# Attention on one core: value products of the fifth step moved into the sixth

## The reference

```python
qkv = jnp.einsum('bnc,dc->bnd', x, qkv_w) + qkv_b
...
attn = jnp.einsum('bhqd,bhkd->bhqk', q, k) * scale
attn = jax.nn.softmax(attn, axis=-1)
out = jnp.einsum('bhqk,bhkd->bhqd', attn, v)
```

## Time and profile before

| | |
|---|---|
| median of 3 runs | 4660.69 us (4658.37 to 4661.96) |
| the profiled execution | 4660.65 us, of which the span is 4658.9 us |
| dense stage | to 1320 us of the span |
| attention groups | 1321 to about 4484 us |
| granted TensorE clock | 0.996 of full speed over the span |

### The profile page before, as it was taken

How to read it: one execution, slowest core, us unless ns; L and a number is a source line. 1 busy time by engine, 2 the same in 40 slices (tenths; PEclk the granted TensorE clock), 3 DMA queues, 4 the chain that set the end, 5 groups by cost and what they waited for, 6 DMA issues and landing times.

```text
span 4658.9 us, 65600 instructions
## 1 busy us (share of the span) xinstructions
PE 4623.1 (99%) x24396; PEld 2958.7 (64%) x24396; DVE 3206.6 (69%) x5313; ACT 2392.8 (51%) x4649; POOL 3176.1 (68%) x1105
## 2 busy tenths in 40 slices
PE   8999999999999999999999999999999999999999
PEld 7888888888755555555555555555555555555567
DVE  5233233333388888888888888888888888888854
ACT  2112121121146666666666666666666666666631
POOL 1121212121268999999999999999999999999910
PEclk9999999999999999999999999999999999999999
DMA  5334353434346666566666666665666666666557
GB/s 176 108 118 138 95 163 93 133 117 135 104 100 135 131 138 135 130 136 135 132 139 133 132 136 134 136 135 128 138 137 132 135 135 132 138 133 136 120 181 259
DMA packets 263425, 629.23 MB, mean 135 GB/s; under 512 B 46788, under 2 KB 83652, under 8 KB 224712
## 3 DMA queue, kind: packets, MB, share of 16 engines
q0 software_dynamic: 36288, 264.26, 27.9%
q1 hardware_dynamic: 226824, 360.85, 27.5%
HBM read 224.96 MB, written 134.74 MB: 77 GB/s over the span
## 4 chain that ended last, share of the span: by engine, by line
PE 62%; POOL 5%; DMA 3%; issue 2%; ACT 1%; DVE 0%; POOLq 0%; DVEq 0%
PE st_ps L1493 20%; PE o_ps L1419 18%; PE mx_ps L1407 18%; POOL p_pair L1121 4%; PE mx_ps L1433 3%; PE st_ps L1441 3%; DMA p_pair<-p_pair 3%; PE mx_ps L1441 1%; ACT p_sb L1197 1%; POOL p_pair L1159 0%; PE mx_ps L1412 0%; POOL o_inv L1115 0%; POOL p_pair L1125 0%; ACT front L1207 0%; DVE y_in L1286 0%
## 5 line engine op out<-in xcount | busy, mean ns | idle before, releaser
L1232 DVE TENSOR_REDUCE unit_max<-mx_ps 128x1 f32<-128x512 f32 x4016 | 2456.4, 682 | 311.1 <-PE mx_ps L1407 309.0
L1197 ACT ACTIVATE p_sb<-st_ps 128x512 f32<-128x512 f32 x4096 | 2063.3, 628 | 860.4 <-PE st_ps L1493 860.3
L1121 POOL TENSOR_TENSOR p_pair<-p_sb 128x2048 f32<-128x2048 f32 x504 | 2433.5, 4875 | 6.7 <-PE mx_ps L1433 3.4
L1419 PE MATMUL o_ps<-p_sb,v_sb 128*32 128x512 f32 x8192 | 986.7, 599 | 0.0
L358 POOL TENSOR_TENSOR h_lo<-h_f,h_hi 128x512 fp32r<-128x512 f32 x128 | 165.3, 1291 | 709.1 <-DVE h_hi L576 709.1
L1419 PEld LDWEIGHTS o_ps<-p_sb,v_sb 128*32 128x32 f32 x8192 | 214.1, 109 | 433.9 <-issue 286.2
L426 ACT ACTIVATE h_f<-rot,b_sb 128x512 f32<-128x512 f32 x128 | 88.1, 689 | 656.0 <-PE rot L627 655.9
L1493 PE MATMUL st_ps<-q_x,k_x 97*128 97x512 f32 x1024 | 401.0, 413 | 1.8 <-ACT p_sb L1197 1.4
L1493 PE MATMUL st_ps<-front 97*128 97x512 f32 x1024 | 399.3, 410 | 1.1 <-ACT p_sb L1197 1.1
L1493 PE MATMUL st_ps<-q_x,front 97*128 97x512 f32 x1024 | 399.1, 410 | 0.0
L1493 PE MATMUL st_ps<-front,k_x 97*128 97x512 f32 x1024 | 398.6, 410 | 0.0
(11 more groups left out here) (124 smaller groups left out, 5922.2 us busy)
## 6 DMA issues: line engine op xcount, KB each, us to landing
p_pair<-p_pair POOLq DMA_DIRECT2D x252, 1024.0 KB, 7.6
xt<-x SPq DMA_DIRECT2D x64, 256.0 KB, 2.7
stage<-w SPq DMA_DIRECT2D x32, 512.0 KB, 4.2
q_hi_d<-qk_hi SPq DMA_DIRECT2D x64, 256.0 KB, 3.1
q_lo_d<-qk_lo SPq DMA_DIRECT2D x64, 256.0 KB, 3.6
k_hi_d<-qk_hi SPq DMA_DIRECT2D x64, 256.0 KB, 2.7
k_lo_d<-qk_lo SPq DMA_DIRECT2D x64, 256.0 KB, 3.4
v_d<-v_out SPq DMA_DIRECT2D x64, 256.0 KB, 2.3
```

The lines of the kernel that those rows point to most:

```text
L1121: pool.tensor_tensor(p_pair[:, slot, :, :], p_sb[:, n % SLOTS, :, :], p_sb[:, (n + 1) % SLOTS, :, :], ALU.add).then_inc(pair_done, 1)
L1197: act.activation(p_sb[:, (L * G * KT + n) % SLOTS, h, :], st_ps[bank(g, m)][:, :], ACT.Exp, scale=SCALE).then_inc(exp_done, 1)
L1232: dve.reduce_max(unit_max[:, n // 4, n % 4:n % 4 + 1], mx_ps[UNIT_PLACE[n] % RING][:, :], AX.X).then_inc(bank_read, 1)
L1419: op = pe.matmul(o_ps[rows, :], v_sb[u][:, kt, rows], p_sb[:, (L * G * KT + n) % SLOTS, h, :], start=(kt == 0), stop=(kt == KT - 1))
```

## The change

Two edits. In `STEPS` the strings of j = 4 and j = 5 are new: step 4 has no V any more and alternates U and S throughout; step 5 keeps its V after four U, and behind it the order is U S S U U S U S S where it was S S U S U U S U S. In `products`, the V of a step whose predecessor has none takes four key tiles (for j = 5: 6 to 9) where the others take two. Nothing is added or taken away, and no wait is of another kind.

```diff
         STEPS = ["USUSUSUVSSUSUUSUS", "USUSUSUVSSUSUUSUS", "USUSUSUVZSSUSUUSUS", "USUSUSUVZSSUSUUSUS",
-                 "USUSUSUVSSUSUUSUS", "USUSUSUVSSUSUUSUS", "USUSUSUVTSSUSUUSUS", "USUSUSUVZSSUSUUSUS"]
+                 "USUSUSUSUSUSUSUS", "USUSUSUVUSSUUSUSS", "USUSUSUVTSSUSUUSUS", "USUSUSUVZSSUSUUSUS"]
...
-                            for kt in (2 * j - 2, 2 * j - 1):
+                            for kt in range(2 * j - (2 if "V" in STEPS[j - 1] else 4), 2 * j):
                                 values(L, g * KT + kt, u, kt)
```

## The result

The changed kernel takes **4704.05 us** (median of 4 runs, 4702.46 to 4704.57), the kernel before 4661.32 us: a ratio of 1.0091, 95% interval 1.0077 to 1.0106. It is 0.9% slower, by 42.7 us; +36.3 us, 4697.0, was the forecast. The profiled execution has a span of 4702.8 us, 43.9 more than before.

The account below looks back on a forecast made before the run. PE's order was taken to bound the kernel; −0.38 + 1.06 − 0.02 = +0.66 us in 63 groups (+41.6), −0.4 for the last group and −4.9 from POOL gave +36.3, 4697.0 us; range 4683 to 4708, 8 times in 10.

Parts of the forecast that it names:

- The bound: In the attention, PE's order of work sets the pace, 49.24 us a group.
- The switch, −0.38 us: At step 4's removed visit, one entry and exit between whole-array and 32-column matmuls is saved, 0.38 us per group.
- Sixteen units, +1.06 us: Between the visits of steps 3 and 5, unit 16 waits for DVE's reduce 12, holding PE 1.06 us per group.
- Behind the long visit, −0.02 us: From step 5's visit to step 6's, the first unit goes two places earlier, the last leaves the edge: −0.02 us.
- What POOL gives back, −4.9 us: Over the attention, PE's longer period gives POOL room, so late joins no longer hold ACT and then PE: −4.9 us.
- The −0.4 us of the last group: The last group has output products instead of units and only saves the switch: −0.4 us.
- A: In steps 4 and 5 the four banks absorb DVE's lag, only the switch counts: faster, 4636 us; chance 5%.
- B: POOL sets the group's period and the extra PE time vanishes in PE's waits: no change, 4661 us; chance 4%.
- C: Key tiles 8 and 9 meet POOL 1.6 us earlier and it stands in their way: 4714 us; chance 6%.

Follow-up runs that it names:

- a_oldtail: Changed kernel with the order behind step 5's visit put back to S S U S U U S U S; 4697.74 us, ratio 1.008.
- b_short: Kernel before with DVE's unit reduces reading 256 of 512 columns and the exponential's scale a hundredth; 4647.26 us, ratio 0.9971.
- b_unit2nd: Kernel before with the first unit and second score behind the visit swapped in all eight steps; 4650.26 us, ratio 0.9976.
- a_short: Changed kernel with DVE's unit reduces reading 256 of 512 columns and the exponential's scale a hundredth; 4642.38 us, ratio 0.9962.
- b_early: Kernel before with S U S U U S U S S behind the visit in all eight steps; 4676.08 us, ratio 1.0028.

## Why the prediction was right

*The bound.* PE's order sets the period. Right: every change of a step on PE came out in the time, until the period fell to about 49.0 us, where late joins at step 2 took part of the gain.

*The switch, −0.38 us.* Right. With the old order behind the visit, steps 4 and 5 of `a_oldtail` are 0.67 us longer than before, and with a hold of 1.04 that leaves 0.37 for the switch. It holds 0.03 us that are not the switch but the edge of the ring at the eighth unit: the prediction took that wait to be without a loss, and `b_short` and `b_unit2nd` show that it was not. `a_short` against `b_short` shows only −0.26, since PE waits for ACT there in two places.

*Sixteen units, +1.06 us.* Right, with 1.04 between short and full reduces, 1.05 by the starts of the two units and of the visit, and 11.53 us for 448 columns, as expected. The wait at the eighth unit in the earlier trace rows, only 0.20 us and next to free, was the row that told it.

*Behind the long visit, −0.02 us.* This is the term that was mis-sized: it is +0.06, by `a_oldtail` against after (49.89 and 49.95). The prediction weighed where the first unit stands and not where the five scores stand, though it had the banks of `st_ps` and ACT's 0.49 us in hand. It is 0.08 us off, and the hold 0.02 the other way: a typical group is 0.71 us longer and not 0.66, which is 63 × 0.05 = 3 of the missing 6.4 us.

*What POOL gives back, −4.9 us.* Half right. The periods of after are level, 49.95 us in nearly every group, where before some took up to 50.1. The long ones of before are long in step 2: it lies over 0.15 us above its median in 7 groups of before and in none of after. Their way is not the one that the prediction gave, through ACT. The chain of before at one of them:

```profile
2806.58 7.89 DMA p_pair<-p_pair
2814.48 0.14 issue
2814.61 1.07 PE mx_ps L1433 x8
```

PE itself waits at the Z of step 2 for the join. With the longer period the joins are there in time. But the mean of before stood 0.09 us above its typical group, and that of after still stands 0.04 above. What is left comes about every eighth group, 0.3 us each time, in both kernels, where the program begins its next turn of eight groups; it was counted as POOL's. The term is −2.8 us, so 2.1 us of give-back were counted too many. The −0.4 us of the last group doesn't show either: the last two copies of `o_raw` lie 53.85 us apart before and 53.87 after. Together this makes 5.7 of the 6.4 us. What is left is smaller than the 2 us by which the four runs of after differ.

*The profiled spans* differ by 43.9 us. 41.2 of them lie between the first and the last copy of `o_raw`, 1375.2 to 4528.0 us against the 1372.5 to 4484.1 of the earlier trace rows. The other 2.7 lie ahead of the attention's second group, mostly in the dense stage, whose program is the same; over the ten profiled kernels the first copy falls anywhere from 1372.5 to 1375.2.

*The rivals.* A and B are excluded by the time and by the eight held units. C did not come: between 1322 and 4428 us ACT never waits for POOL's pairs in after. Without DVE's lag the merger does save, as A had it, but 4.9 us (`a_short` against `b_short`) and not 24.

The rule on the drain from the Trainium skill, page "TensorEngine Tiling (Array Packing)", section Tiling Modes, fits the price of the switch, 0.35 to 0.38 us; that it is a drain no run here shows. Its section Performance Considerations says that emptying PSUM may become the bottleneck, and means the output of tiled matmuls. Here it was the output of the untiled ones that DVE couldn't empty in time, as soon as the tiled visits no longer gave it a pause.

## What to carry to other kernels

Where two engines are tied by a ring of buffers, work of a third kind between them may be what lets the slower one catch up: merging such visits saves a switch and spends the slack. Look for the short wait that costs next to nothing yet, the last one before the pause: it tells how many items the ring bears, and the price of more is the difference of the two periods, item by item (here 0.60 − 0.47 us, eight times). And when an order is written by hand, check every ring that it runs past: swapping one pair in each of the eight steps took 12 us off here, and `b_early`, which also sets two scores later, put 14 on.

## What the runs showed of the hardware that was not expected

The reciprocal that inverts the sums waited for its DMA in 27 groups of after, 37.2 us in all and up to 1.8 each, where it waited once, for 0.4 us, before. DVE comes to it about 8.2 us after SP has issued the transfer, where it was 9.3 before, but that alone is not the cause: `a_short` comes to it after 5.9 us and waits only 3 times. The transfer itself is late. By the updates of its semaphore it lands 5.2 us after its issue in before (median of 61 groups); in after it takes more than 8 us in 26 of 61 groups, mostly 9.2 to 10.0. In 23 of these 26 POOL had issued a join ahead of it, and in only 2 of the other 35. Before, the join came behind it in 60 of 61. The transfer has 8 KB, the join 1024 KB. The two issues, before:

```profile
2528.01 0.60 SPq L963 DMA_DIRECT2D sum_t<-sum_raw  x1
2528.39 0.88 POOL L1125 DMA_DIRECT2D p_pair<-p_pair  x1 [0.30 <-ACT p_sb L1197]
```

and after:

```profile
2544.62 0.88 POOL L1125 DMA_DIRECT2D p_pair<-p_pair  x1 [0.30 <-POOL p_pair L1121]
2545.74 0.60 SPq L963 DMA_DIRECT2D sum_t<-sum_raw  x1
```

With the longer period the small transfer is often issued behind the large one, and lands late when it is. No run changes the order of these two alone, so this is read from the traces and not shown by an experiment. It cost nothing: from the first score of step 4 to that of step 7 the groups with the wait and those without it take the same 18.24 us.

And a busy share can hide a loss completely: DVE's idle time stayed at 311 to 318 us and PE's share at 99% while PE lost 1.04 us in every group.
